# Two of eight experts for every token: rows sorted by expert through DRAM, in groups of 256, instead of every expert over every row

## The chip, the cores and the metric

The kernel runs on one core of a Trainium2 chip. A core has TensorE (PE in the profile; PEld is its weight load), VectorE (DVE), ScalarE (ACT), GpSimd (POOL) and SyncE (SP, which here only issues DMAs). The metric is the device time of one execution in microseconds (us), lower is better.

## What is computed

Four layers over a batch of 16 sequences of 256 tokens of width 128 (4096 rows, 32 tiles of 128 rows), each as x + layernorm(f(...)): a softmax attention, a block with a second softmax attention and a mixture of experts, an attention with second-power weights and decay, and a mixture with capacities. The change is about the mixture in the second layer (D = 128, hidden width F0 = 256, NE = 8 experts and a shared one):

```python
logits = h2 @ router_w
topw, topi = top_k(softmax(logits), 2);  topw = softmax(topw)
combine = sum(one_hot(topi, 8) * topw[..., None], axis=1)
shared = swiglu(h2, sh_gate, sh_up, sh_down)
gate = einsum('td,edf->etf', h2, e_gate);  up = einsum('td,edf->etf', h2, e_up)
eout = einsum('etf,efd->etd', silu(gate) * up, e_down)
moe_out = shared + einsum('etd,te->td', eout, combine)
```

`combine` is zero for six of the eight experts of every token.

## The kernel before

The program is one block per engine, each a list of steps written out by hand; engines meet only at semaphores, and nothing is reordered. There are five stages. `soft_layers` runs both softmax attentions, 32 steps of one sequence (tiles and semaphores end in S in the profile). `gated_layer` is the mixture above. `power_layer` is the third layer, 16 steps of 8 units, one head pair each (names end in P). `route` and `capped_mixture` are the last layer. A stage's first and last pieces are put into its neighbour's steps through tables of "guests": the key says after which step or unit, the value which piece. So the first steps of power (transposes, Q and K, the decays of sequences 0 and 1) are guests in the last part of the mixture, and the end of the mixture's last block is drained in power's first steps.

`gated_layer` before: 8 blocks (NBLK) of 512 rows. For a block the router's logits are formed and the two best experts found (`route`, small VectorE operations on 128x32 elements), then the block goes through all nine experts. The hidden width of an expert is cut in two chunks of 128, so a block has 18 units and the stage 144. A unit is:

- PE: three f16 matmuls of 512 columns into gate_ps and three into up_ps (each product of f32 numbers is made of three products of f16 halves, `PARTS`), L2121 and L2126. After both chunks of an expert, `down` (L2100) sends 24 f16 matmuls of 128 columns into down_ps.
- ACT: SiLU of gate_ps (gsg, L2187), later the high f16 half of the product (ghid, L2174).
- DVE: the product with up_ps (gprod, L2333), and per expert four additions weighted by `comb` (gacc, L2298).
- POOL: the low half (ghid, L2044).

At a block's end VectorE takes the layer norm's moments, GpSimd a power for the root (grs, L2039), VectorE applies it (gtmp, L2313) and adds to X. The weights of all experts are brought from DRAM, lifted and split in halves during `soft_layers` (27 pieces: gate, up and down of nine).

In `power_layer` the PE sends scores and decays of a unit (score_psP, decay_psP), VectorE takes the magnitude (AP, L1396, waits for the scores), ScalarE squares it and takes the decay's exponential, GpSimd multiplies the two (PTP, L982), and PE multiplies by V.

The last layer already uses indirect DMAs: GpSimd gathers token rows into xe by an index (L2442) and scatters results into expert_outputs (L2449), 128 rows each.

## Time and profile before

| | us |
|---|---|
| median of 3 runs | 1215.96 (1214.22 to 1217.85) |
| span of the profiled execution | 1221.8 |
| PE busy | 1117.0 |
| VectorE busy | 995.4 |
| ScalarE busy | 854.8 |
| GpSimd busy | 660.7 |

The profiled execution has a span of 1221.8 us, 5.8 us above the median of the timed runs; no other time of it is given, so this span is taken as its own time. Busy is the union of an engine's instructions. PE's busy time includes modelled ends, and the granted clock (1.00 is the full 2.4 GHz, 0.5 is 1.2 GHz) says how fast it was allowed to be.

### The profile page before, as it was taken

Reading aid. Unit: us, or ns where it says so; the run is one execution under the profiler, and the core shown is the slowest. Engines: PE = TensorE matmul, PEld = TensorE weight load, DVE = VectorE, ACT = ScalarE, POOL = GpSimd, SP = SyncE. Lnnn points to the kernel's source line nnn. Section 1 sums busy time; section 2 is a strip of 40 time slices with the busy share of each in tenths; the row PEclk is TensorE's granted clock in tenths of the full one; section 3 lists DMA queues with packets and bytes.
Section 4 is the critical chain, followed back from the end, with each engine's and each line's share of the span. In section 5 each row is a group of like instructions: output and inputs, shape, how many; then the busy total and the mean of one; then the engine's idle time right before and its main releaser. Section 6 shows DMA issues by size and latency. Waiting matters only on the chain. (4 is left out here: it accounts for less than half of the span.)

```text
span 1221.8 us, 33461 instructions
## 1 busy us (share of the span) xinstructions
PE 1117.0 (91%) x11750; PEld 627.2 (51%) x11750; DVE 995.4 (81%) x2706; ACT 854.8 (70%) x1830; POOL 660.7 (54%) x692
## 2 busy tenths in 40 slices
PE   5999999999999999999999999998999999947786
PEld 2344444444444444666656555555566665524552
DVE  4899999999899995788998889789899999771223
ACT  1788888888888887655555655688799998642214
POOL 3243344455333320666555666577788887725563
PEclk9999999999999998999999999999899999958998
DMA  4111111111111110000000000001212122041117
...
DMA packets 83459, 48.91 MB, mean 40 GB/s; under 512 B 17431, under 2 KB 80352, under 8 KB 83296
## 3 DMA queue, kind: packets, MB, share of 16 engines
...
## 5 line engine op out<-in xcount | busy, mean ns | idle before, releaser
L627 DVE TENSOR_REDUCE mxsS<-scoreS 128x2 f32<-128x512 f32 x512 | 328.6, 684 | 38.0 <-PE scoreS L766 32.7
L515 ACT ACTIVATE PTS<-stS 128x512 f32<-128x512 f32 x512 | 283.5, 591 | 52.6 <-PE stS L770 52.1
L2044 POOL TENSOR_TENSOR ghid<-gprod,ghid 128x512 f16<-128x512 f32 x144 | 165.7, 1158 | 141.4 <-ACT ghid L2174 140.3
L766 PE MATMUL scoreS<-QK 31*128 31x256 f16 x1024 | 173.3, 279 | 23.0 <-DVE mxsS L627 11.4
L982 POOL TENSOR_TENSOR PTP<-PTP,EP 128x512 f32<-128x512 f32 x128 | 163.2, 1286 | 51.0 <-ACT PTP L1210 50.9
L770 PE MATMUL stS<-QK 32*128 32x256 f16 x1024 | 169.6, 276 | 1.3 <-ACT PTS L515 1.3
L2174 ACT ACTIVATE ghid<-gprod 128x512 f16<-128x512 f32 x144 | 90.3, 627 | 94.8 <-DVE gprod L2333 94.0
L691 PE MATMUL pvS<-PTS,Vx 128*32 128x256 f32 x2048 | 140.3, 392 | 0.3
L1396 DVE TENSOR_SCALAR AP<-score_psP 128x768 int32<-128x768 int32 x128 | 121.5, 949 | 10.6 <-PE score_psP L1554 9.9
L766 PEld LDWEIGHTS scoreS<-QK 31*128 31x128 f16 x1024 | 53.8, 93 | 145.3 <-DVE mxsS L627 94.0
L1210 ACT ACTIVATE PTP<-AP,epsP 128x768 f32<-128x768 f32 x128 | 119.2, 932 | 7.1 <-DVE AP L1396 6.4
L388 POOL TENSOR_TENSOR rsS<-veS,halfS 128x2 f32<-128x2 f32 (+1 forms) x32 | 28.0, 874 | 171.1 <-DVE veS L595 90.6
L2121 PE MATMUL gate_ps<-ghT,split 128*128 128x512 f16 x432 | 116.9, 379 | 3.5 <-ACT gsg L2187 3.4
L2126 PE MATMUL up_ps<-ghT,split 128*128 128x512 f16 x432 | 116.8, 379 | 3.3 <-DVE gprod L2333 3.3
L2333 DVE TENSOR_TENSOR gprod<-gsg,up_ps 128x512 f32<-128x512 f32 x144 | 96.0, 681 | 23.2 <-ACT gsg L2187 18.1
L2100 PEld LDWEIGHTS down_ps<-split,ghid 128*128 128x128 f16 x1728 | 102.0, 98 | 17.6 <-issue 3.5
L2100 PE MATMUL down_ps<-split,ghid 128*128 128x128 f16 x1728 | 108.2, 219 | 0.0
L2187 ACT ACTIVATE gsg<-gate_ps 128x512 f32<-128x512 f32 x144 | 84.4, 586 | 28.0 <-PE gate_ps L2121 26.8
L1220 ACT ACTIVATE EP<-decay_psP 128x512 f32<-128x512 f32 x128 | 75.6, 591 | 20.1 <-PE decay_psP L1536 19.5
L691 PEld LDWEIGHTS pvS<-PTS,Vx 128*32 128x32 f32 x2048 | 54.1, 110 | 49.6 <-issue 21.9
L2126 PEld LDWEIGHTS up_ps<-ghT,split 128*128 128x128 f16 x432 | 41.4, 98 | 56.7 <-DVE gprod L2333 8.0
L2298 DVE SCALAR_TENSOR_TENSOR gacc<-down_ps,gcomb,gacc 128x128 f32<-128x128 f32 x224 | 62.6, 341 | 0.0
...
## 6 DMA issues: line engine op xcount, KB each, us to landing
...
tokens<-XB SPq DMA_DIRECT2D x16, 128.0 KB, 3.1
...
```

What stands on the lines that cost most here:

```text
L515: act.activation(PT[:, n % NPT, :], st_ps[:, (NS * t + n) % 3, :], ACT.Exp, scale=SCALE).then_inc(s_exp, 1)
L627: dve.tensor_reduce(mxs[:, u // 4, :, at], score_ps[:, n % 2, :].rearrange("p (c s) -> p c s", c=TC), AX.X, ALU.max).then_inc(s_max, 1)
L691: last = pe.matmul(pv_ps[32 * j:32 * j + 32, q], Vx[:, t % 3, c, 4 * g + j, :], PT[:, (4 * g + (j ^ 2)) % NPT, S * c:S * c + S], start=(c ...
L766: scored = pe.matmul(score_ps[:, k, cols], QK[part, new, g, 0, rows], QK[part, new, g, 1, :], start=True, stop=True)
L770: turned = pe.matmul(st_ps[:, (NS * t + n) % 3, cols], QK[part, old, g, 1, rows], QK[part, old, g, 0, :], start=True, stop=True)
L982: eng.tensor_tensor(w, w, E[:, n % NE, :], ALU.mult).then_inc(s_wd if n % NU in MULT_BY_DVE else s_wp, 1)
L1210: act.activation(PT[:, n % NW, :], A[:, n % NA, :], ACT.Square, bias=eps[:, 0:1]).then_inc(s_sq, 1)
L1396: dve.tensor_scalar(A[:, n % NA, :].bitcast(I32), score_ps[:, n % 2 * WU:n % 2 * WU + WU].bitcast(I32), 0x7FFFFFFF, None, ALU.bitwise_and) ...
L2044: pool.tensor_tensor(hid[:, n // FC % NHID, 1, c, :], prod[:, n % NPROD, :], hid[:, n // FC % NHID, 0, c, :], ALU.subtract).then_inc(s_hid, 1)
L2100: last = pe.matmul(down_ps[:, x % 2, t * D:(t + 1) * D], hid[:, x % NHID, lh, c, t * P:(t + 1) * P], down_w[:, lw, x % EX, c, :], start=(c ...
L2121: last = pe.matmul(gate_ps[:, n % 2, :], gate_w[:, lw, e, cols], hT[:, n // NQ % 2, lh, :], start=(k == 0), stop=(k == 2))
L2126: last = pe.matmul(up_ps[:, n % 3, :], up_w[:, lw, e, cols], hT[:, n // NQ % 2, lh, :], start=(k == 0), stop=(k == 2))
```

## The change

Blocks are now groups of 256 rows. The shared expert still runs over all rows in order: 16 units. For the eight others, each row is written twice to a DRAM table (`sorted0` for blocks 0 to 3, `sorted1` for 4 to 7), at a place that VectorE works out from the two chosen experts: rows of one expert stand together, and every expert begins at a multiple of 256. 4096 entries in up to 8 runs need at most 23 groups of 256, and all 23 are always run, for each half: 46 sorted units. So the stage has 62 units, each of 256 rows and the whole hidden width.

A sorted unit is loaded from the table by SyncE (gsin), transposed by PE (gturn_ps), split in halves by ScalarE and VectorE (ghTs), multiplied, and its result goes through ScalarE (gob) to the DRAM table `mixed`. Its expert is read by PE from SBUF into a register (TENSOR_LOAD), and the weights' addresses are computed from it with register instructions (ISA in the rows below). 64 indirect DMAs on GpSimd scatter the rows, 64 gather the results back, 8 for every block of 512 rows. VectorE then adds two results for every row with their weights. The third factor, `down`, is now f32 (weights not split, product not split), four f32 matmuls a unit.

The tables are first set to zero in 24 DMAs of up to 256 KB in the soft steps. The rows' scaling (squares, root, rows) moves to GpSimd in the soft steps 20 to 31, and the logits of blocks 0 to 3 and the first choice of experts into the last soft step. Blocks 0 to 3 are gathered and added in the mixture's last units (48 to 61), blocks 4 to 7 in power's steps 1 to 8.

On PE, in the middle of the mixture (gate_ps, up_ps and down_ps as above, split holds the f16 weights), two units of 128 hidden columns and 512 rows were:

```order
L2121 MATMUL gate_ps<-ghT,split 128x512 x3
L2126 MATMUL up_ps<-ghT,split 128x512 x3
L2121 MATMUL gate_ps<-ghT,split 128x512 x3
L2126 MATMUL up_ps<-ghT,split 128x512 x3
L2100 MATMUL down_ps<-split,ghid 128x128 x24
```

One sorted unit now is this, with down of the unit two before it and the transposes of the group two after it:

```order
L2233 TENSOR_LOAD gowner_139
L2233 ISA x2
L2295 ISA
L2295 MATMUL ggate_ps<-ghTs,split 128x256 x2
L2295 ISA
L2295 MATMUL ggate_ps<-ghTs,split 128x256
...
L2295 MATMUL gup_ps<-ghTs,split 128x256
L2263 ISA
L2263 MATMUL gdown_ps<-down_w,gprod 128x128
L2263 ISA
L2263 MATMUL gdown_ps<-down_w,gprod 128x128 x3
L2247 MATMUL gturn_ps<-cst,gsin 128x128 x2
```

Between the ISA rows stand in all 12 gate and up matmuls of 256 columns with 8 register instructions; with the load, its 2 and the 2 of down a unit has 13 instructions that were not there.

On POOL, at the mixture's end and in power's first two steps, stood (ghid is the low half, yP are power's rows):

```order
L2044 TENSOR_TENSOR ghid<-gprod,ghid 128x512 x10
L982 TENSOR_TENSOR PTP<-PTP,EP 128x512 x3
L1053 TENSOR_SCALAR yP<-X,mvP,rsP 128x128
L982 TENSOR_TENSOR PTP<-PTP,EP 128x512 x3
L1053 TENSOR_SCALAR yP<-X,mvP,rsP 128x128
L982 TENSOR_TENSOR PTP<-PTP,EP 128x512 x5
```

and now, from power's step 1 on, a gather stands after every second product:

```order
L2139 DMA ggot_late<-mixed,gidx_106 128x128
L975 TENSOR_TENSOR PTP<-PTP,EP 128x512 x2
L2139 DMA ggot_late<-mixed,gidx_106 128x128
L975 TENSOR_TENSOR PTP<-PTP,EP 128x512 x2
L1045 TENSOR_SCALAR yP<-X,mvP,rsP 128x128
L2139 DMA ggot_late<-mixed,gidx_106 128x128
L975 TENSOR_TENSOR PTP<-PTP,EP 128x512 x2
```

On POOL ahead of that, at the mixture's beginning, all 64 scatters stand in a row, with one root between them:

```order
L2128 DMA sorted<-gy,gidx_105 5888x128 x4
L2095 TENSOR_TENSOR girs<-gms,ghalf 128x4
L2128 DMA sorted<-gy,gidx_105 5888x128 x28
L2128 DMA sorted<-gy,gidx_106 5888x128 x32
```

The diff, cut to its core:

```diff
+MOE_PARTS = (4, 4)
+SLOTS = 256
...
+    SHARED, SORTED = NB, sum(groups)
+    UNITS = SHARED + SORTED
...
+        def expert(pe, n):
+            if n < SHARED:
+                return NE
+            h, j = group(n - SHARED)
+            if j == 0:
+                pe.wait_ge(s_rank, RANKED * (h + 1))
+            owners[n] = pe.value_load(owner[h][0:1, j:j + 1], min_val=0, max_val=NE)
+            return owners[n]
+
+        def columns(e, width, start, size):
+            if isinstance(e, int):
+                return slice(e * width + start, e * width + start + size)
+            return ds(e * width + start, size)
+
+        def sorted_turn(pe, s):
+            pe.wait_ge(s_sin[s % RING], 16 * (s // RING + 1))
...
+            reach(pe, s_slo, s)
+            for c in range(TC):
+                last = pe.transpose(turn_ps[:, c * P:(c + 1) * P], sin[:, s % RING, c, :], ident)
+            last.then_inc(s_sturn, 1)
 
         def down(pe, x):
-            pe.wait_ge(s_hid, FC * (x + 1))
+            pe.wait_ge(s_prod, x + 1)
...
+            for t in range(TC):
                 for c in range(FC):
-                    for k, (lh, lw) in enumerate(PARTS):
-                        last = pe.matmul(down_ps[:, x % 2, t * D:(t + 1) * D],
-                                         hid[:, x % NHID, lh, c, t * P:(t + 1) * P], down_w[:, lw, x % EX, c, :],
-                                         start=(c == 0 and k == 0), stop=(c == FC - 1 and k == 2))
+                    last = pe.matmul(down_ps[:, x % 2, t * D:(t + 1) * D],
+                                     prod[:, x % NPROD, c * SLOTS + t * P:c * SLOTS + (t + 1) * P],
+                                     down_flat[:, columns(e, FC * D, c * D, D)], start=(c == 0), stop=(c == FC - 1))
             last.then_inc(s_down, 1)
...
+            def hidden(n):
+                e = expert(pe, n)
+                if n < SHARED:
+                    pe.wait_ge(s_lo, n // 2 + 1)
+                else:
+                    pe.wait_ge(s_slo, n - SHARED + 1)
...
+                reach(pe, s_sg, n - 1)
+                for weight, ps, full in ((gate_w, gate_ps, s_gate), (up_w, up_ps, s_up)):
+                    if ps is up_ps:
+                        reach(pe, s_prod, n - 1)
+                    for c in range(FC):
+                        for k, (lw, lh) in enumerate(PAIRS):
...
+                            last = pe.matmul(ps[:, n % 2, c * SLOTS:(c + 1) * SLOTS],
+                                             weight[:, lw, columns(e, F0, c * P, P)], rows,
+                                             start=(k == 0), stop=(k == 2))
+                    last.then_inc(full, 1)
...
+        def scatter(pool, h, k):
+            c, t = k // len(tiles[h]), k % len(tiles[h])
+            if k == 0:
+                pool.wait_ge(s_zero, 3 + 16 * ZERO_PIECES)
+                pool.wait_ge(s_rank, RANKED * h + PLACED)
...
+            pool.indirect_dma_start(tables[h], bass.IndirectOffsetOnAxis(ap=idx[h][:, c, t:t + 1], axis=0),
+                                    y[:, tiles[h].start + t, :], None).then_inc(s_sorted[h], 16)
+
+        def gather(pool, b, k):
+            h, c, i = part_of_block(b), k // TB, k % TB
+            if k == 0:
+                stores(pool, h)
...
+            pool.indirect_dma_start(results_of(b)[:, c, i, :], None, results[h],
+                                    bass.IndirectOffsetOnAxis(ap=idx[h][:, c, t:t + 1], axis=0)).then_inc(arrival(b)[0], 16)
...
+        def add_shared(dve, x):
+            dve.wait_ge(s_down, x + 1)
+            a = XB[:, TC * x:TC * x + TC, :].rearrange("p c d -> p (c d)")
+            dve.scalar_tensor_tensor(a, down_ps[:, x % 2, 0:TC * D], 1.0 / LIFT, a, ALU.mult, ALU.add).then_inc(s_acc, 1)
+
+        def add_chosen(dve, b, c):
...
+            for i in range(TB):
+                t = b * TB + i
+                last = dve.scalar_tensor_tensor(XB[:, t, :], results_of(b)[:, c, i, :], W[:, c, t:t + 1], XB[:, t, :],
+                                                ALU.mult, ALU.add)
+            last.then_inc(s_sum, 1)
...
+            for n in range(UNITS):
+                if n < 4:
+                    soft.drain_vector(dve, n)
...
+                product(n)
...
+                if n == 2:
+                    rank(dve, 0)
+                if n == 14:
+                    choose(dve, 1)
+                if n == 16:
+                    rank(dve, 1)
...
+                if n >= SHARED - 1 and n + 2 < UNITS:
+                    sorted_low(n + 2 - SHARED)
...
+        def load(sp, s):
+            h, j = group(s)
+            if j == 0:
+                sp.wait_ge(s_sorted[h], 16 * 2 * len(tiles[h]))
...
+def groups_of(h):
+
+    return (2 * MOE_PARTS[h] * 512 + NE * (SLOTS - 1)) // SLOTS
```

`rank` is 13 VectorE operations on PE's running counts: each expert's number of rows, its first group, each row's place, and each group's expert.

## Rows read from the trace of the kernel before

**Rows 1.** The page: busy time by engine.
```profile
PE 1117.0 (91%) x11750; PEld 627.2 (51%) x11750; DVE 995.4 (81%) x2706; ACT 854.8 (70%) x1830; POOL 660.7 (54%) x692
```

**Rows 2.** Busy time in stretches: mixture, power, the last layer (busy us of each engine, clock).
```profile
486.00:793.00 307.00, 297.33 (x2708) 187.01 (x2704) 265.86 (x815) 182.24 (x358) 189.46 (x175) 1.00 0.02 4
793.00:1059.00 266.00, 257.84 (x3460) 155.59 (x3458) 240.72 (x574) 232.12 (x487) 213.53 (x196) 0.98 0.17 45
1059.00:1222.00 163.00, 111.83 (x578) 68.46 (x576) 63.24 (x294) 54.14 (x144) 78.20 (x85) 0.82 0.32 91
```

**Rows 3.** Who waited for whom, 486 to 793 us: total, times, longest.
```profile
PEld gate_ps L2121 <- ACT gsg L2187: 8.1, 11, 1.8
PEld up_ps L2126 <- DVE gprod L2333: 8.0, 10, 1.5
```

**Rows 4.** PE in order of time in the mixture: start, length, instruction, count.
```profile
485.96 0.82 PE L2121 MATMUL gate_ps<-ghT,split 128*128 128x512 f16 x3
...
494.90 1.50 PE L2100 MATMUL down_ps<-split,ghid 128*128 128x128 f16 x24
496.24 0.81 PE L2121 MATMUL gate_ps<-ghT,split 128*128 128x512 f16 x3
...
602.25 0.81 PE L2121 MATMUL gate_ps<-ghT,split 128*128 128x512 f16 x3
602.90 0.81 PE L2126 MATMUL up_ps<-ghT,split 128*128 128x512 f16 x3
...
792.75 0.38 PE L1519 MATMUL decay_psP<-cstb 128*128 128x512 bf16 x1
```

**Rows 5.** The chain that ended last: f32 matmuls and a gather's landing.
```profile
1110.75 2.40 DMA xe<-tokens,idx_in
...
1137.43 3.57 PE cps L2496 x32
```

**Rows 6.** Groups of instructions of the whole trace: count, busy us, mean ns.
```profile
L2333 DVE TENSOR_TENSOR gprod<-gsg,up_ps 128x512 f32<-128x512 f32 x144 | 96.0, 681 | 23.2 <-ACT gsg L2187 18.1 <-PE up_ps L2126 3.3 <-DVE gsel L2253 0.4
L2187 ACT ACTIVATE gsg<-gate_ps 128x512 f32<-128x512 f32 x144 | 84.4, 586 | 28.0 <-PE gate_ps L2121 26.8
L714 PE MATMUL miscS<-cst,yS 128*128 128x128 f32 x64 | 14.7, 314 | 0.7 <-DVE router L1728 0.7
L604 DVE SCALAR_TENSOR_TENSOR HLS<-miscS,bq,HLS 128x256 f16<-128x256 f32 x16 | 7.6, 475 | 2.7 <-ACT HLS L486 2.7
```

**Rows 7.** GpSimd in order of time: indirect DMAs, with the idle time ahead of each.
```profile
1109.50 0.94 POOL L2442 DMA_INDIRECT xe<-tokens,idx_in  x1 [0.30 <-issue]
1110.75 0.94 POOL L2442 DMA_INDIRECT xe<-tokens,idx_in  x1 [0.30 <-issue]
```

**Rows 8.** DMA issues: count, size, us to landing.
```profile
experts<-in_L_ffn_e_gate_dram SPq DMA_DIRECT2D x8, 128.0 KB, 2.3
```

**Rows 9.** VectorE in order of time, the third product of the mixture.
```profile
490.87 0.69 DVE L2333 TENSOR_TENSOR gprod<-gsg,up_ps 128x512 f32<-128x512 f32 x1 [0.91 <-ACT gsg L2187]
```

**Rows 10.** Busy time in power's steps 1 to 4 and 5 to 8.
```profile
809.60:876.00 66.40, 60.68 (x807) 36.21 (x807) 60.78 (x143) 55.17 (x111) 52.38 (x48) 0.95 0.15 41
876.00:942.40 66.40, 65.83 (x881) 41.13 (x880) 60.88 (x151) 59.16 (x131) 53.73 (x51) 0.97 0.20 53
```

**Rows 11.** Lines 1323 and 2241: durations in ns, least, median, most.
```profile
L1323 DVE TENSOR_TENSOR ynP<-farP,rcP x16: 291/426/1187, 827.0 to 1070.5; 128x128 f32<-128x128 f32 x16
L1323 DVE TENSOR_TENSOR ynP<-misc_bP,rcP x15: 290/291/292, 823.6 to 1058.4; 128x128 f32<-128x128 f32 x15
...
L2241 DVE TENSOR_TENSOR gsc<-gsc,cst x8: 181/990/991, 480.2 to 744.7; 128x32 f32<-128x32 f32 x8
```

**Rows 12.** Groups in power's steps 0 to 8: count, busy us, mean ns.
```profile
L982 POOL TENSOR_TENSOR PTP<-PTP,EP 128x512 f32<-128x512 f32 x68 | 86.7, 1285 | 30.9 <-ACT PTP L1210 30.7
L2039 POOL TENSOR_TENSOR grs<-gve,ghalf 128x4 f32<-128x4 f32 x1 | 1.0, 1025 | 0.0
...
L2313 DVE TENSOR_SCALAR gtmp<-gacc,gmv,grs 128x128 f32<-128x128 f32 x4 | 2.3, 578 | 0.0
L2298 DVE SCALAR_TENSOR_TENSOR gacc<-down_ps,gcomb,gacc 128x128 f32<-128x128 f32 x8 | 2.2, 336 | 0.0
```

**Rows 13.** Busy time in the second half of the soft stage.
```profile
250.00:460.00 210.00, 202.71 (x2374) 98.91 (x2370) 193.89 (x443) 181.81 (x398) 77.95 (x99) 1.00 0.17 40
```

1110 lines of the change are left out of this document (646 added, 464 removed).

## The prediction

> **What bounds the kernel now.** I read the page first, then the stretches, then the mixture's waits and PE's own order in it. The page has PE busy for 1117.0 of 1221.8 us [rows 1], but the three stretches behind the soft stage differ: in the mixture PE is busy 297 of 307 us, while ScalarE and GpSimd are busy 182 and 189 [rows 2]. The longest waits of PE there sum to 16 us [rows 3]. So the mixture is bound by PE's columns. Its length is from the first gate_ps at 485.96 to power's first matmul at 792.75, 306.8 us [rows 4]. Three matmuls of 512 columns pass in 0.65 us and 24 of 128 columns in 1.34 us (494.90 to 496.24) [rows 4], that is 217 and 56 ns each, with the weight loads hidden. One of the 144 units costs 6 x 0.217 + 12 x 0.056 = 1.97 us, all of them 284 us; the other 23 us are seven blocks' transposes and logits, power's first guests and waits. In power, the reader should see three engines close together: PE 257.8, VectorE 240.7, ScalarE 232.1 of 266 us, GpSimd 213.5 [rows 2]. What leaves the mixture for power does not fall on an idle engine.
>
> **The change: PE's units.** A matmul of 256 columns is bounded by the two rows at 56 and 217 ns [rows 4]; by its columns it is 0.109. Gate and up have 12: 1.31 us. Down is four f32 matmuls of 128 columns, eight records; 32 such records passed in 3.57 us, 0.112 each [rows 5]: 0.90. A shared unit is 2.21 us. A sorted unit has two f32 transposes more, 64 of which took 14.7 us, 0.23 each [rows 6]: 2.67 us of array time. 16 x 2.21 + 46 x 2.67 = 158 us against 284: the columns saved are worth 126 us. It is that little because 46 groups are always run, where two experts a row would fill 32.
>
> **The register instructions.** No row shows one. Below, they are bounded by nothing: the 22 matmuls and 22 weight loads of a sorted unit need at most 1.23 us to issue, at the 28 ns an instruction that the 48 of down show (1.34 us for 24 pairs [rows 4]), so 13 register instructions hide beside 2.67 us as long as each takes under 0.11. Above, the nearest row of an instruction that fetches something before it can go is GpSimd's 0.30 us of issue ahead of each indirect DMA [rows 7]: 1.23 + 13 x 0.30 = 5.1 us a unit. They can't overlap waits much, since several carry the unit's semaphore waits. I take 0.13 each, near the lower end since twelve of thirteen read no memory, so a sorted unit is 1.23 + 1.69 = 2.92 us. The first transfer to a register is the one that may be long.
>
> The Trainium skill (DMA: Bandwidth & Descriptors, "Latency and other measured facts") gives a floor of about 600 ns for such a load of a register from a tensor. With the other twelve at 0.11 an estimate by that page would be 3.2 us a unit, some 11 us more in all. No row here shows it.
>
> **The start: GpSimd's scatters.** Let G be the time of the first gate_ps. PE has 16 shared units less two downs that come later (33.6), the fronts of four blocks (four transposes and 12 tiny matmuls, at most 0.92 + 0.67, so 6.4) and 1 us of the soft stage's drain: it is through at G + 41. The third product ended at 490.87 + 0.69, G + 5.6 [rows 9]; behind it stand 12 steps of rank, each like a small VectorE operation of 181 to 990 ns [rows 11], which I put at 0.28: G + 9. Then GpSimd issues 32 scatters, one every 1.25 us (1109.50 to 1110.75 [rows 7]), with a root of 1.0 [rows 12] between: the last goes at G + 49. A gather landed 2.40 us after its issue [rows 5], a load of 128 KB takes 2.3 [rows 8], two transposes and two halves 1.4 (0.48 for the low half [rows 6]). The first sorted unit starts at G + 55. PE waits 14 us. The second half's scatters start when rank(1) is done, about G + 62, end at G + 102 and are ready at G + 108; PE comes there after 23 units, at G + 122. They are hidden by the first half's units, and cost nothing unless these shrink below 2.3 us.
>
> **The end: GpSimd's gathers.** The last result of the first half is stored three units late, about G + 131. 32 gathers are 40 us, the roots and power's first rows 8, waits inside 4: G + 183. PE comes to unit 60, which needs the last of them, at about G + 190. Covered, by 7 us; at 2.67 us a unit by nearly nothing, so PE can't gain all of its own speed.
>
> Mixture: 55 + 46 x 2.92 = 189, and for power's guests and their waits 13 as now (306.8 less 283.7 of units and 7 x 1.6 of fronts, plus the two downs that are drained later): 202. Saved: 104 us.
>
> VectorE and ScalarE have room in it: per sorted unit 0.68 + 0.48 and 0.59 + 2 x 0.4 us [rows 6].
>
> **Power's steps 1 to 8.** These took 132.8 us, with GpSimd busy 52.4 + 53.7 and VectorE 60.8 + 60.9 [rows 10]. GpSimd gets 32 gathers of 1.25 and four roots, less the one of before: 106 + 43 = 149 us. VectorE loses about 5 us of block 7's moments and norm (gtmp alone is 2.3 [rows 12]) and gets this four times, and 32 additions. An addition of before is 0.34 us [rows 12], but it read PSUM; the new one reads two operands from SBUF. Line 1323 shows both kinds: from PSUM 290 to 292 ns, with both in SBUF 291 to 1187, median 426 [rows 11]. For each block I take 2.7 + 1.5: 122 - 5 + 4 x 9.2 = 154 us. Neither fits in 132.8. At the 97 to 99% that the busiest engine reaches (PE 65.8 of 66.4 [rows 10]), 158 us: lost 25. If the additions never wait it is 14, if each does for 0.9 us, 45.
>
> **The soft stage.** Four blocks' fronts for one on PE, 4.8 us. VectorE's six sums of squares (0.68 each, as gprod of the same shape [rows 6]) go to an engine busy 194 of 210 us and mostly fit [rows 13]; the zeroing DMAs fit, since nothing waits for them there. Nine weight pieces fewer on ScalarE and GpSimd give nothing: PE, at 203 of 210, is the bound. Lost: 5 us.
>
> The last layer is as before, with weights brought later, under power's last steps.
>
> Sum: -104 + 25 + 5 = -74. From the profiled 1221.8, 1148; the median of the runs is 5.8 lower, so **1142 us**. Own range: 1116 (2.67 us a unit less what the gathers hold back, power at 14, a shorter stall) to 1165.
>
> **Rivals.** (a) Registers free and power cheap: 1110 to 1116, as just worked out. For it, PE's issue of 28 ns an instruction; against it, the engines' sums in power. (b) Registers at 0.17 to 0.25 us: units of 3.4 to 4.5 us, 1166 to 1215. (c) GpSimd's issue slows under load. All 28 + 28 indirect DMAs of before ran with VectorE busy 63 of 163 us [rows 2]; now it is busy 80% and more beside them. At 2.0 us each the first stall grows by 24 and power by 18: 1184. The second kind of line 1323 [rows 11] says that the two engines do get in each other's way. The Trainium skill (SBUF — State Buffer, "SBUF: two separate sides") says that a VectorE operation that takes the shared port pair keeps GpSimd from writing its descriptors. By that rule the DMAs' own durations would stretch, and not only VectorE's; no row here shows it. (d) Slower than before: register instructions at the issue gap, 0.30 us each, nothing hidden. 46 x (5.13 - 2.92) = 102: 1244 us. It decides from 0.25 us each on, where a unit is 4.5 us. Against it, only one in thirteen reads memory. (e) The columns are saved but PE falls to 1.2 GHz whenever it waits: in power's steps 1 to 4 the clock was 0.95 with PE busy 91% [rows 10]. With PE at 84% there and a 14 us stall in the mixture it may cost 5 to 15 us, inside the range.
>
> **Numbers.** Forecast with (e) 0.5, (a) 0.12, (b) 0.14, (c) 0.12, (d) 0.1, else 0.02. The range 1112 to 1190 leaves out (d), half of (b)'s upper part and a part of (a). A difference of 0.3%, 4 us, is what can be told here. Faster 0.87, same 0.02, slower 0.11.
>
> **What would show it.** In the profile after: gate_ps to gate_ps of neighbouring sorted units 2.9 us apart, with PE's gaps marked as issue; a wait of about 14 us at unit 16 for a DMA, with GpSimd's 32 scatters 1.25 us apart ahead of it; the whole mixture near 202 us; power's steps 1 to 8 near 158 us with GpSimd and VectorE over 93% busy and PE waiting for them. I'd be wrong if units were over 3.5 us, if the indirect DMAs stood over 1.5 us apart, or if a step of power stayed at 16.6 us.

## The result and the profile after

The changed kernel takes **1180.9 us** (median of 4 runs, 1178.53 to 1187.95), the kernel before, run beside it, 1215.1 (4 runs, 1213.49 to 1217.85): a ratio of 0.972, 95% interval 0.968 to 0.976. It is faster, as forecast, and inside the range, but by 34 us where 74 had been forecast.

The profiled execution took 1178.53 us, its span is 1176.7. The page has this row in place of [rows 1]:

```profile
PE 1030.3 (88%) x10524; PEld 615.7 (52%) x10524; DVE 887.7 (75%) x2262; ACT 757.2 (64%) x1638; POOL 644.3 (55%) x707
```

PE lost 1226 matmuls and 87 us of busy time. Busy time in stretches, in the columns of [rows 2]: the mixture, the power layer, and the piece from power's step 15 to the end:

```profile
501.00:699.00 198.00, 165.28 (x1460) 149.35 (x1458) 115.24 (x300) 79.68 (x182) 112.00 (x122) 0.93 0.33 96
703.00:968.00 265.00, 244.87 (x2620) 143.78 (x2624) 227.24 (x538) 185.91 (x385) 206.48 (x189) 0.76 0.16 42
1012.00:1177.00 165.00, 119.13 (x779) 74.26 (x778) 75.65 (x320) 66.03 (x165) 88.30 (x94) 0.84 0.34 96
```

The column behind the engines is the clock that TensorE was granted: in power it was 0.98 before [rows 2] and is 0.76 now. PE in order of time, as in [rows 4]:

```profile
500.82 0.83 PE L2295 MATMUL ggate_ps<-hTf,split 128*128 128x256 f16 x6
...
542.41 0.82 PE L2295 MATMUL ggate_ps<-hTf,split 128*128 128x256 f16 x6
...
546.64 0.70 PE L2208 MATMUL gfront_ps<-gmask,gones 128*128 128x128 bf16 x16
559.29 0.69 PE L2247 MATMUL gturn_ps<-cst,gsin 128*128 128x128 f32 x2 [11.95 <-DMA gsin<-sorted]
561.15 0.66 PE L2247 MATMUL gturn_ps<-cst,gsin 128*128 128x128 f32 x2 [1.18 <-DVE ghTs L2549]
562.25 1.46 PE L2295 MATMUL ggate_ps<-ghTs,split 128*128 128x256 f16 x6 [0.43 <-issue]
...
601.98 0.82 PE L2295 MATMUL ggate_ps<-ghTs,split 128*128 128x256 f16 x6
...
604.40 0.82 PE L2295 MATMUL ggate_ps<-ghTs,split 128*128 128x256 f16 x6
...
699.10 0.58 PE L1519 MATMUL decay_psP<-cstb 128*128 128x512 bf16 x1 [0.42 <-DMA MP<-partsP]
```

The reader should see the mixture's two ends, 500.82 and 699.10; a sorted unit every 2.42 us (601.98 to 604.40) with no gap; and the stall ahead of the first sorted unit, 542.41 to 562.25. GpSimd's first scatters, which that stall waits for:

```profile
514.55 1.22 POOL L2128 DMA_INDIRECT sorted<-gy,gidx  x1 [0.18 <-issue]
516.08 0.96 POOL L2128 DMA_INDIRECT sorted<-gy,gidx  x1 [0.30 <-issue]
517.35 0.96 POOL L2128 DMA_INDIRECT sorted<-gy,gidx  x1 [0.31 <-issue]
```

Where the time went, from the marks of [rows 4] and the starts of power's steps (a step is timed from VectorE's first operation on score_ps). The second profile of the kernel before is the experiment before_again:

| stretch, us | before | before, second profile | after |
|---|---|---|---|
| up to the first gate_ps | 486.0 | 492.3 | 500.8 |
| mixture | 306.8 | 306.3 | 198.3 |
| power, to the start of step 15 | 252.0 | 251.0 | 313.1 |
| step 15 to the end | 177.0 | 165.2 | 164.5 |
| span | 1221.8 | 1214.8 | 1176.7 |

Against the first profile that is +14.8, -108.5, +61.1 and -12.5, together -45.1; against the second +8.5, -108.0, +62.1 and -0.7, together -38.1. The mixture gave what was forecast; power took back more than half of it.

**Power's steps 0 to 11**, the stretch that all experiments are compared in. The kernel before, then the kernel after:

```profile
795.40:994.80 199.40, 191.43 (x2556) 116.69 (x2554) 182.41 (x438) 175.07 (x373) 162.09 (x150) 0.97 0.17 46
```
```profile
703.00:962.20 259.20, 239.07 (x2540) 140.19 (x2540) 221.55 (x521) 180.68 (x375) 200.90 (x185) 0.76 0.16 42
```

TensorE runs the same matmuls (the counts differ by records that are missing). It is busy with them for 47.6 us more and waits 12.2 us more (20.1 for 8.0): four fifths of the 59.8 us stand in its busy time, with the granted clock at 0.76 in place of 0.97, that is, with more of the matmuls at the lower of its two clock levels, 1.2 GHz. That says where the time stands, and not what a held clock would give back. Steps 12 to 14 have none of the new work and take 50.0 us in both.

### The profile page after: what moved, and what is told of

The parts are those of the page before. It is cut to its first block and busy times, and to the rows that moved or that the text cites. A ratio compares the mean times of both kernels' runs of the same rounds, so it can differ in the third digit from the quotient of the medians.

```text
span 1176.7 us, 30894 instructions
## 1 busy us (share of the span) xinstructions
PE 1030.3 (88%) x10524; PEld 615.7 (52%) x10524; DVE 887.7 (75%) x2262; ACT 757.2 (64%) x1638; POOL 644.3 (55%) x707
## 5 line engine op out<-in xcount | busy, mean ns | idle before, releaser
L760 PE MATMUL scoreS<-QK 31*128 31x256 f16 x1024 | 171.3, 280 | 33.5 <-DVE mxsS L621 14.8
L1396 DVE TENSOR_SCALAR AP<-score_psP 128x768 int32<-128x768 int32 x128 | 121.7, 951 | 21.6 <-PE score_psP L1555 20.6
L2128 POOL DMA_INDIRECT sorted<-gy,gidx x64 | 61.6, 963 | 32.6 <-issue 32.6
L2263 PE MATMUL gdown_ps<-down_w,gprod 128*128 (+1 forms) x496 | 68.4, 284 | 2.1 <-issue 1.1
L2361 ACT ACTIVATE ghTs<-gturn_ps,norm 128x256 f16<-128x256 f32 x46 | 21.8, 474 | 74.7 <-PE gturn_ps L2247 74.7
L2263 PEld LDWEIGHTS gdown_ps<-down_w,gprod 128*128 128x128 f32 x496 | 62.9, 199 | 3.8 <-issue 3.0
L2545 DVE TENSOR_TENSOR gprod<-gsg,gup_ps 128x512 f32<-128x512 f32 x62 | 42.6, 686 | 25.1 <-PE gup_ps L2295 19.1
L1541 PE MATMUL score_psP<-QK 31*128 31x128 f16 x512 | 58.3, 242 | 0.0
L1537 PE MATMUL decay_psP<-MP 32*128 32x128 bf16 x512 | 58.2, 242 | 0.0
L1520 PE MATMUL decay_psP<-cstb 128*128 128x512 bf16 x128 | 57.9, 452 | 0.0
L2356 ACT ACTIVATE gsg<-ggate_ps 128x512 f32<-128x512 f32 x62 | 37.1, 598 | 30.5 <-PE ggate_ps L2295 30.5
L1555 PE MATMUL score_psP<-QK 31*128 31x128 f16 x256 | 39.9, 241 | 18.8 <-DVE AP L1396 18.0
```

The source lines that it names most:

```text
L760: scored = pe.matmul(score_ps[:, k, cols], QK[part, new, g, 0, rows], QK[part, new, g, 1, :], start=True, stop=True)
L1396: dve.tensor_scalar(A[:, n % NA, :].bitcast(I32), score_ps[:, n % 2 * WU:n % 2 * WU + WU].bitcast(I32), 0x7FFFFFFF, None, ALU.bitwise_and) ...
L1541: pe.matmul(score_ps[:, o:o + P], QK[band, t % 3, g, 1, rows], QK[band, t % 3, g, 0, rows], start=True, stop=True)
L2128: pool.indirect_dma_start(tables[h], bass.IndirectOffsetOnAxis(ap=idx[h][:, c, t:t + 1], axis=0), y[:, tiles[h].start + t, :], None).then_ ...
L2263: last = pe.matmul(down_ps[:, x % 2, t * D:(t + 1) * D], prod[:, x % NPROD, c * SLOTS + t * P:c * SLOTS + (t + 1) * P], down_flat[:, colum ...
```

## The experiments

The table has power's steps 0 to 11 of every kernel: their length, TensorE's busy time and waits in it, its mean granted clock, VectorE's busy time, and "excess", which is worked out from the trace: by how much VectorE's operations were longer than the shortest of their line and shape in the whole trace, summed where it is over 0.15 us. Runs with an interval had three rounds, the others one execution; each ratio is to the kernel before as it ran beside that kernel. The length of these steps differs between single executions by more than small effects: static and zero_act change nothing in power and have 248.3 and 259.6 us, the kernel after 259.2. Differences under some 11 us between two lengths are no evidence by themselves.

| kernel | run, us | ratio to before, 95% | length | PE busy | PE waits | clock | VectorE | excess |
|---|---|---|---|---|---|---|---|---|
| before | 1215.1 | 1 | 199.4 | 191.4 | 8.0 | 0.97 | 182.4 | 12.1 |
| before_again | 1216.6 | | 198.4 | 191.5 | 6.9 | 0.97 | 181.6 | 11.3 |
| after | 1180.9 | 0.972 (0.968 to 0.976) | 259.2 | 239.1 | 20.1 | 0.76 | 221.6 | 31.1 |
| fill1 | 1187.1 | 0.973 (0.965 to 0.980) | 267.4 | 242.0 | 25.4 | 0.84 | 225.8 | 33.5 |
| fill2 | 1174.2 | 0.964 (0.956 to 0.972) | 250.8 | 235.7 | 15.1 | 0.96 | 219.1 | 26.9 |
| fill_odd | 1181.0 | 0.973 (0.967 to 0.979) | 252.0 | 236.3 | 15.7 | 0.91 | 220.4 | 29.7 |
| no_late | 1156.3 | | 234.5 | 214.9 | 19.6 | 0.86 | 199.4 | 16.0 |
| no_gather | 1172.9 | | 251.0 | 232.8 | 18.2 | 0.79 | 211.4 | 20.6 |
| no_add | 1182.4 | | 256.2 | 237.2 | 19.0 | 0.76 | 210.0 | 26.0 |
| spread | 1198.7 | 0.982 (0.977 to 0.987) | 271.0 | 240.1 | 30.9 | 0.76 | 228.2 | 38.0 |
| spread_fill | 1200.3 | 0.986 (0.983 to 0.990) | 272.4 | 245.7 | 26.7 | 0.90 | 230.5 | 39.9 |
| before_burst | 1231.3 | | 219.8 | 205.5 | 14.3 | 0.90 | 198.4 | 20.2 |
| before_gather | 1231.9 | | 214.0 | 201.1 | 12.9 | 0.92 | 192.2 | 21.5 |
| zero_act | 1170.1 | 0.962 (0.958 to 0.967) | 259.6 | 237.9 | 21.8 | 0.76 | 217.7 | 27.0 |
| zero_fill | 1163.1 | 0.959 (0.953 to 0.965) | 249.4 | 234.2 | 15.2 | 0.96 | 219.2 | 27.1 |
| zero_fill_os | 1168.8 | 0.960 (0.955 to 0.966) | 263.3 | 241.4 | 21.9 | 0.93 | 222.2 | 37.2 |
| light | 1167.8 | 0.960 (0.955 to 0.965) | 256.3 | 232.2 | 24.1 | 0.79 | 225.1 | 34.1 |
| light_fill | 1167.3 | 0.959 (0.955 to 0.964) | 255.3 | 238.2 | 17.1 | 0.94 | 225.3 | 33.1 |
| half_scatter | 1174.1 | | 259.9 | 234.7 | 25.2 | 0.78 | 223.4 | 33.0 |
| static | 1166.4 | | 248.3 | 223.4 | 24.9 | 0.82 | 217.4 | 26.9 |

A correction to texts below: block b's additions stand in power step 2b-5 and its normalization in 2b-4, so for the late blocks 4 to 7 in steps 3, 5, 7, 9 and 4, 6, 8, 10; the gathers in 2b-7 and 2b-6, steps 1 to 8. Only step 11 has no work of its own, and it shows: 16.1 us in the kernel after. Step 0 has the additions of block 3.

### Clock or occupation: fill1, fill2, no_late

fill1 adds one matmul of 512 columns to each unit of the affected steps, fill2 two:

```
-                for _ in range(AGAIN if t >= NB - 2 else t == 0):
+                for _ in range(AGAIN if t >= NB - 2 else t <= 11):               # fill1
+                for _ in range(AGAIN if t >= NB - 2 or t <= 11 else 0):          # fill2
```

> One more matmul of 512 columns per unit (0.22 us, its result is overwritten) in power's steps 1 to 11; nothing is left out. Clock theory: the 61 us lost in power are mainly TensorE running at 1.2 GHz after it has waited for VectorE; the extra work keeps it busy, time at 1.2 GHz in power falls from 133 us to under 60, steps 4 to 11 fall from 20 to 27 us to 17 to 20, and the kernel is 15 to 35 us faster than the changed one (1145 to 1165). Occupation theory: VectorE and GpSimd set the steps, the clock only follows; the extra matmuls change nothing or cost up to 20 us (1180 to 1200).

> Two more such matmuls per unit in power's steps 0 to 11. Clock theory: hardly any time at 1.2 GHz in power, but 3.5 us of TensorE a step more, so steps that VectorE does not fill (9 to 11) take 18 to 20 us: 1150 to 1170. Occupation theory: TensorE's work now passes that of VectorE, 1195 to 1225.

no_late drops the late blocks' gathers and keeps one column of their additions:

```
             t = (b - first_block[h]) * TB + i
+            if b >= first_block[1]:
+                return
             pool.indirect_dma_start(results_of(b)[:, c, i, :], None, results[h], ...)
...
+                if b >= first_block[1]:
+                    last = dve.scalar_tensor_tensor(XB[:, t, 0:1], XB[:, t, 0:1], W[:, c, t:t + 1], XB[:, t, 0:1], ...)
+                    break
```

> Leaves out the 32 gathers of blocks 4 to 7 and all but one column of their additions, so the chosen experts' results are missing in half the rows; moments and norm of these blocks stay in power. Clock theory and occupation theory both expect a large gain in steps 1 to 8; the clock theory expects steps 9 to 11 to be 16 us too, since they were slow without any work of their own, power near 275 us in all and the kernel at 1125 to 1140. If steps 9 to 11 stay at 20 to 25 us, what slows them is something else.

Steps 0 to 11 of fill2, then of no_late:

```profile
705.60:956.40 250.80, 235.67 (x2723) 128.89 (x2721) 219.09 (x522) 180.50 (x376) 201.51 (x186) 0.96 0.17 44
```
```profile
705.80:940.30 234.50, 214.85 (x2541) 128.43 (x2540) 199.40 (x498) 177.99 (x375) 166.40 (x153) 0.86 0.14 37
```

fill2 brings the clock back to 0.96. Its 183 matmuls more, at the 0.217 us of [rows 4], are 40 us of TensorE; what is left of its busy time is 196, where 191 is the kernel before. So TensorE's own matmuls took 43 us less and the fillers 40 more; the length fell by 8, which one execution can't show. The run of 1174.2 is between the ranges of both theories, and its interval overlaps that of the change. fill1 holds the clock half way and gains nothing that can be told (1187.1, as the theory of occupation had it). Neither run gives the price of the clock alone, since the fillers take TensorE's time.

no_late takes 25 of the 60 us, and its run of 1156.3 missed the range of 1125 to 1140. The clock still falls without that work (0.86), and 35 of the 60 us stay. Block 3's additions in step 0 and all blocks' moments and normalization stand there still; no run leaves them out, so what the 35 us are is not shown.

### Which engine: no_gather and no_add

no_gather leaves out the gathers only (the additions read the token row itself), no_add reduces the additions only.

> The 32 late gathers (blocks 4 to 7) are left out, their additions stay and read the token row itself: GpSimd has 8 issues of about 1.25 us fewer per block, VectorE as much work as in the changed kernel. Theory A: the slow steps 3, 5, 7 stay at 23 to 27 us and the run at 1170 to 1181 us. Theory C (GpSimd): steps as in no_late, 16 to 22 us, and 1153 to 1160 us.

> The 32 late gathers stay, their additions are reduced to one column: VectorE is relieved of 8 additions a block, GpSimd not. Theory A: as no_late, 1153 to 1162 us. Theory C: as the changed kernel, 1175 to 1185 us.

```profile
705.40:956.40 251.00, 232.82 (x2540) 137.00 (x2540) 211.37 (x522) 179.36 (x375) 167.53 (x153) 0.79 0.13 35
```
```profile
710.10:966.30 256.20, 237.21 (x2540) 139.16 (x2538) 209.99 (x498) 179.63 (x375) 200.38 (x185) 0.76 0.16 42
```

no_gather's run of 1172.9 is in theory A's range and no_add's of 1182.4 in theory C's, so neither alone is the cause: without the gathers 8 us go, without the additions 3, without both 25. The 8 and the 3 are too small for single executions; that the two don't add up to 25 is the reading. In no_add the steps with four gathers still take 17 to 27 us, with GpSimd busy up to 21 of 27; in no_gather a step with additions takes 20.2 with VectorE busy 20.0, and the step behind it up to 25.9 at a clock of 0.53. The kernel after has the same in steps 9 and 10:

```profile
901.40:921.50 20.10, 17.56 (x235) 10.66 (x238) 19.86 (x56) 15.41 (x34) 14.10 (x13) 0.97 0.12 32
921.50:946.10 24.60, 24.60 (x210) 14.50 (x210) 17.38 (x44) 15.70 (x34) 15.46 (x14) 0.54 0.09 24
```

TensorE waits for 2.5 us in step 9; the low clock comes in step 10, where it waits for nothing and is busy for the whole of 24.6 us.

no_add shows a second thing. Its VectorE executes as many operations as no_late's (x498), of the same sizes, and is busy 10.6 us longer. The operations themselves are longer. The kernel after, VectorE and GpSimd in order of time in step 7:

```profile
852.64 1.04 POOL L2139 DMA_INDIRECT ggot_late<-mixed,gidx  x1 [0.16 <-ACT PTP L1204]
852.66 0.30 DVE L1332 TENSOR_TENSOR farP<-misc_bP,farP 128x144 f32<-128x144 f32 x1
852.99 0.25 DVE L1319 RECIPROCAL rcP<-farP 128x16 f32<-128x16 f32 x1
853.28 3.08 DVE L1321 TENSOR_TENSOR ynP<-farP,rcP 128x128 f32<-128x128 f32 x1
...
853.70 2.49 POOL L975 TENSOR_TENSOR PTP<-PTP,EP 128x512 f32<-128x512 f32 x2
```

The operation onto yn reads both operands from SBUF; its twin that reads PSUM takes 0.29 every time [rows 11]. Here it takes 3.08 us and ends at 856.36, just behind GpSimd's gather and **two** products (852.64 to 856.19). Beside it the operation of 852.66, which reads PSUM, is not stretched. [rows 11] has the same line at up to 1.19 us in the kernel before, one product's length. The Trainium skill (SBUF — State Buffer, "Who interferes with whom") says that a VectorE operation with both inputs in SBUF and a GpSimd one that reads SBUF exclude each other for a whole instruction. The trace agrees, and goes further: here VectorE did not get its turn between three GpSimd instructions in a row.

### Each cost by itself in the kernel before: before_burst, before_gather

Steps 7 and 11 of the kernel before are steady at 16.1 us. before_burst gives VectorE 16 operations more in each:

```
+                    if t in (7, 11) and u % 2 == 1:
+                        for i in range(4):
+                            dve.scalar_tensor_tensor(spare[:, i, :], cst[:, 0:P], cst[:, 0:1], cst[:, 0:P], ALU.mult, ALU.add)
```

> The kernel before, with 16 extra VectorE operations of 128x128 (onto a tile of their own) in each of the power steps 7 and 11, four ahead of units 1, 3, 5 and 7; both steps lie in its steady part, where a step takes 16.1 us with VectorE busy 15.2 and TensorE 16.0 at 2.4 GHz. The additions take about 0.35 us each, so VectorE has 20.8 us of work in such a step. Theory of the clock: the step gets 4 to 6 us longer by the wait, TensorE's granted clock falls, and with it this or the next step gets another 4 to 9 us, so 8 to 15 us for each of the two bursts and 16 to 30 us in the run (1232 to 1246). Theory of occupation alone: 20.8 to 21.5 us for the step, 16.1 for the next, 10 us in the run (1225).

before_gather gives GpSimd four gathers more in each:

```
+                    if t in (7, 11) and u % 2 == 1:
+                        ...
+                        pool.indirect_dma_start(spare[:, u // 2, :], None, dram["L0_ffn_wo"],
+                                                bass.IndirectOffsetOnAxis(ap=first_row[:, 0:1], axis=0))...
```

> The kernel before, with four extra indirect gathers of 128 rows on GpSimd in each of the power steps 7 and 11 (ahead of the products of units 1, 3, 5, 7, into tiles of their own); VectorE and TensorE get no work more. GpSimd has 14.0 us of work in such a step of 16.1, plus 4 x 1.25 = 19.0. Theory of the shared way into SBUF: GpSimd comes behind, its products run back to back, VectorE's operations with two SBUF operands stretch (from 0.3 to 1 to 3 us each), so VectorE's busy time in the step grows from 15.2 to 17 to 19 us without an operation more, and the step takes 19 to 24 us. Theory that GpSimd's products are buffered and that only VectorE's own work counts: the step stays at 16.1 to 17 and VectorE at 15.2.

before_burst, step 6 and step 7; then before_gather, step 6 and step 7:

```profile
897.10:913.20 16.10, 16.00 (x221) 9.95 (x220) 15.38 (x41) 15.19 (x35) 14.19 (x15) 1.00 0.22 54
913.20:939.70 26.50, 22.97 (x221) 13.41 (x220) 23.19 (x56) 16.80 (x36) 15.88 (x15) 0.68 0.15 38
```
```profile
903.90:920.00 16.10, 16.00 (x221) 9.94 (x220) 15.36 (x40) 15.19 (x35) 14.17 (x15) 1.00 0.19 52
920.00:942.70 22.70, 19.80 (x221) 12.03 (x220) 19.54 (x39) 15.92 (x36) 19.98 (x19) 0.77 0.30 57
```

Each burst costs 10.4 us, in its own step; the next is 16.0 again. VectorE gets 8 us more, of which 5.5 are the 16 operations at their shortest (0.34) and the rest excess; TensorE waits 3.4 us more, and is busy 7.0 more at a clock of 0.68. That is the theory of the clock, 8 to 15 us a burst, with a run of 1231.3 just under its range. The four gathers cost 6.6 us (the second time 7.0), and the VectorE column is the point: with not one operation more it rises from 15.4 to 19.5 (17 to 19 had been expected, and 19 to 24 us for the step). From the trace of that step, in order of time:

```profile
925.87 0.99 POOL L1093 DMA_INDIRECT spareP<-in_L_ffn_wo_dram,first_rowP  x1 [0.16 <-issue]
...
926.23 3.43 DVE L1285 TENSOR_TENSOR partsP<-restP,partsP 16x256 bf16<-16x256 f32 x1
...
926.88 2.48 POOL L986 TENSOR_TENSOR PTP<-PTP,EP 128x512 f32<-128x512 f32 x2
```

This is the same picture as in the kernel after, produced by gathers alone. In step 11 of the same run it was the operation of L1283, a cast that reads one operand from SBUF: 3.34 us where its shortest is 0.28, again across a gather and two products. So it isn't only the operations with two. The theory that only VectorE's own work counts is out.

These prices can't be added up for the change. Eight steps with four gathers at 6.8 and four with 8 additions at half a burst, 5.2, would be 75 us; no_late took out just this work, and 25 us went. What a gather or an addition costs in a step that is already slow is less than in a steady one.

### Three tries at relief: spread, fill_odd, light, each with its filled twin

spread puts one tile's addition in each unit of the step, and moments and normalization in the next (with GpSimd's root two units later):

```
-                    after.update({(t, 3): tail(("add0", b)), (t, 5): tail(("add1", b)), (t, 7): tail(("moments", b)),
-                                  (t + 1, 3): tail(("apply", b))})
+                    after.update({(t, u): tail((f"tile{u}", b)) for u in range(8)})
+                    after.update({(t + 1, 1): tail(("moments", b)), (t + 1, 5): tail(("apply", b))})
```

> The late additions one tile per unit over all eight units of steps 3, 5, 7, 9, the moments in unit 1 and the normalization in unit 5 of the step behind; nothing is left out. Theory A (VectorE's burst): VectorE is busy 22.8 us of step 7 and 17.0 of step 8 (39.8 for the pair, against 30.4 for a pair of the kernel before), so steps 3 to 10, which took 186.9 us in the changed kernel, can come down toward 4 x 39.8 = 159; expected 165 to 175, a run of 1160 to 1171 us, and pairs of like steps (20 and 21 us) in place of 26 and 21. Theory B (the sum of the work on VectorE counts, however it lies, and TensorE's clock follows the waits): steps 3 to 10 stay at 180 to 190 and the run at 1176 to 1188. Theory C (GpSimd's gathers hold up the products): as B.

> As spread, and two extra matmuls in each unit of power steps 0 to 10, as in fill2. If the clock still falls with the additions spread (theory A with the clock as a second cause), this takes another 5 to 10 us: 1150 to 1163 us. If spreading alone keeps TensorE at 2.4 GHz, the filler costs what it did in step 11 of fill2 (2.8 us a step where TensorE is the bound, less where VectorE is): 0 to 10 us slower than spread. Theory B: 1170 to 1180, as fill2.

Theory A is out: steps 3 to 10 take 186.1 us (187.0 in the kernel after), as B and C had it, which this run can't tell apart. But at 1198.7 the run missed every range. It is slower than the kernel after by 18, by a later start of power (711.0 for 703.0) and by steps 1 and 11, which are 7 us longer each, step 11 at a clock of 0.64. Why the clock falls there is not shown. Excess grew to 38.0; that operations in more places meet GpSimd more often fits this, and is not tested. spread_fill ran at 1200.3, with the clock at 0.90, excess at 39.9 and steps 3 to 10 at 191.3. That is out of the ranges of theories A and B; it is 2 us above spread, as in the third case, but that case had the clock held without fillers, and it was not. On this placement two fillers a unit gained nothing.

fill_odd puts three matmuls a unit where VectorE is the bound and one elsewhere:

```
-                for _ in range(AGAIN if t >= NB - 2 else t == 0):
+                for _ in range(AGAIN if t >= NB - 2 else 3 if t in (3, 5, 7, 9) else int(t <= 10)):
```

> The changed kernel with three extra matmuls in each unit of steps 3, 5, 7 and 9 (where VectorE is the bound) and one in the others up to 10. In steps 0 to 11 TensorE's busy time grew from 191.4 to 239.1 us with the same matmuls and its waits from 8.0 to 20.1; fill2 took back the clock (busy 235.7) but its 183 extra matmuls cost 39 us. If the fillers of the odd steps go into time that VectorE takes anyway (steps of 22.5 to 24.5) and one holds the clock in the even ones (17.4 to 18.5), steps 3 to 10 take 160 to 170 us and the run 1160 to 1172. If the clock falls in the even steps, as in fill1: 1178 to 1190.

Steps 3 to 10 take 175.1 us, no better than fill2's 174.3 and outside the 160 to 170 hoped for; the run of 1181.0 is that of the kernel after and lies in the second range. The clock was 1.00 in steps 4 and 10 and 0.84 and 0.85 in 6 and 8. A filler placed by the bound isn't better than an even one.

light takes work off GpSimd (and has zero_act's edit, below):

```
-                    if u == 4 and has(t + 3):
+                    if u == 4 and has(t + 3) and t not in LIGHT:
                         normalized(pool, t + 3, 0)
...
+            def normal(t, c):
+                act.activation(y[:, c, :], batch_rows(t)[c], ACT.Identity, bias=nm[:, c:c + 1], scale=rs[:, c:c + 1])...
```

> zero_act, and in power steps 1 to 9 the two normalizations of incoming rows and the two of outgoing rows (128x128, 0.86 to 0.95 us each on GpSimd) are done by ScalarE with a bias that VectorE makes (two tiny operations a step, 0.15 us each); nothing is left out. GpSimd's work in a step with four gathers falls from 19.0 to 15.4 us, under the 16.1 of TensorE. If GpSimd's being behind is what stretches VectorE's operations: stretched time (29.5 us more than in the kernel before over steps 0 to 11) halves at least, steps 3 to 10 take 160 to 172 us instead of 183, and the run 1148 to 1162. If VectorE's work or the clock alone decide: within 5 us of zero_act's 1170.

> light with two extra matmuls in each unit of power steps 0 to 11. Beside zero_fill's 1163.1. If GpSimd's being behind sets the addition steps: steps 3 to 10 (24.2, 18.9, 24.7, 18.9, 24.6, 18.9, 21.3, 21.2 in zero_fill) come to 20 to 22 and 18.9, 8 to 16 us less: 1147 to 1156 us. If not: 1160 to 1167.

The 29.5 us in the text of light were counted by another rule; by that of the table the excess grew by 19.0 us (31.1 for 12.1). light, steps 0 to 11:

```profile
692.80:949.10 256.30, 232.19 (x2540) 136.22 (x2540) 225.09 (x538) 191.94 (x409) 172.42 (x151) 0.79 0.16 42
```

GpSimd is relieved by 29 us (zero_act has 201.0), and the excess does not fall: 34.1, where zero_act has 27.0. The run is 1167.8 for zero_act's 1170.1, not 1148 to 1162, and light_fill is not under zero_fill. So relieving GpSimd over a whole step does not shorten VectorE's operations, and that part of the theory falls. In both long operations shown above a gather and two products stood back to back; that this order decides it is argued from them, not tested.

### The soft stage: zero_act

```
-                soft.sync(sp, {2 + k: functools.partial(gated.zeroed, sp, k) for k in range(ZERO_PIECES)})
+                soft.sync(sp, {})
...
+                soft.scalar(act, {**{(2 + k, 3): functools.partial(gated.zeroed, act, k) for k in range(ZERO_PIECES)}, ...
```

> The changed kernel with its 22 zeroing transfers started from ScalarE's queue in place of SyncE's; all else as it was. Start of the mixture was 14.8 us later than in the kernel before (500.8 and 486.0), 9.3 of it by the end of step 19, in which time the zeroing runs. Theory A (the small shift and spread transfers of QK queue behind the 256 KB ones of SyncE): 6 to 10 us of it go, mixture's start at 491 to 495 and a run 5 to 12 us under the changed kernel's, if the power steps don't change. Theory B (16 DMA engines are busy with the zeroing, whatever queue it comes from): the start stays at 499 to 502. Theory C (ScalarE pays for the issues, 22 x 0.1 us or more): 500 to 506.

TensorE's waits for the small transfers onto QK, 0 to 465 us (total, times, longest): before, after, zero_act.

```profile
PE scoreS L766 <- DMA QK<-nmS: 7.0, 10, 1.2
```
```profile
PE scoreS L760 <- DMA QK<-nmS: 14.4, 17, 1.5
```
```profile
PE scoreS L760 <- DMA QK<-nmS: 6.4, 13, 1.2
```

Theory A: the waits are back at what they were before, and the mixture starts 9.7 us earlier:

```profile
491.15 0.83 PE L2295 MATMUL ggate_ps<-hTf,split 128*128 128x256 f16 x6
```

This is no chance of one execution: in the eleven kernels that zero from SyncE the mixture starts at 499.2 to 505.3 us, in the five that zero from ScalarE at 489.2 to 491.6, and in the kernel before and its variants at 485.6 to 492.3. The bytes are the same; the small transfers on SyncE's queue had waited for the 256 KB ones ahead of them in that queue. The Trainium skill (DMA: Bandwidth & Descriptors, "Queues, rings and completion order") says that a DMA engine takes turns between the queues that it has work for; the trace agrees, since the transfers moved to another queue and the waits went. The run is 1170.1, a ratio of 0.962 to the kernel before. zero_twice, the changed kernel with each zeroing transfer started twice, was meant for the same question and has no result.

### The first stall and the registers: half_scatter, static

half_scatter leaves out the second choice's 16 scatters of the first half; static takes the expert's number from the program instead of a register:

```
-            moved(0, range(4, 2 * len(tiles[0])))
+            moved(0, range(4, len(tiles[0])))                                    # half_scatter
...
-            owners[n] = pe.value_load(owner[h][0:1, j:j + 1], min_val=0, max_val=NE)
+            owners[n] = (n - SHARED) % NE                                        # static
```

> The 16 scatters of the second choice of the first half are left out (those rows of the sorted table stay zero), so the first table is whole about 20 us earlier; the transfers of the table, the units and everything behind stay. If the scatters at 1.26 us each make TensorE wait 17.6 us before unit 16: that wait goes to 0 to 2 us, the mixture takes 179 to 184 us instead of 198.3, and the run 1160 to 1170. If the table's own transfer or the ranking sets it: wait and mixture as they were.

> The expert of a sorted group comes from a fixed number instead of a register loaded from SBUF (the groups get a wrong expert's weights; work and order are the same). The sorted units took 2.42 us each with register loads of about 0.3 us on TensorE's queue. If those are hidden, as the back-to-back matmuls say: 2.40 to 2.42 us per unit and a run within 5 us of the changed kernel's. If a part shows: 2.1 to 2.35 us per unit, 3 to 14 us over 46 units.

half_scatter, PE: the last shared unit and the first sorted one:

```profile
546.92 0.82 PE L2295 MATMUL ggate_ps<-hTf,split 128*128 128x256 f16 x6
554.37 1.46 PE L2295 MATMUL ggate_ps<-ghTs,split 128*128 128x256 f16 x6 [0.46 <-issue]
```

7.45 us between them where the kernel after has 19.84: 12.4 us of the stall were scatters, not all of it. What is left is led by the chain of ranking and count (TensorE waits 1.7 us for gmask) and the turn of the first rows (three waits, 3.0 us). The mixture took 188.0 us, not 179 to 184. The run is one execution at 1174.1, above its range, with a soft stage 4.6 us longer than that of the kernel after, and says little by itself.

static, PE:

```profile
603.13 0.82 PE L2295 MATMUL ggate_ps<-ghTs,split 128*128 128x256 f16 x6
...
605.55 0.82 PE L2295 MATMUL ggate_ps<-ghTs,split 128*128 128x256 f16 x6
```

2.42 us a unit, as with registers, whose load shows in the kernel after, from the group that reads gowner (count, least/median/most in ns):

```profile
L2233 PEldq TENSOR_LOAD <-gowner x46: 296/305/511, 561.2 to 688.9; - x46
```

A load of 0.3 us is hidden entirely by the matmuls already queued. static's run of 1166.4 is outside its range of 5 us, and by its steps (248.3 us for 259.2) that comes from power, which holds no register: TensorE is busy there 15.7 us less at a clock of 0.82. It is the scatter from one execution to the next, and the size of doubt on every single run here. The Trainium skill (DMA: Bandwidth & Descriptors, "Latency and other measured facts") gives about 600 ns for such a load; here it was 305.

### The last layer: before_again

> The kernel before as it is, for a second profile. In its first one TensorE's instructions in the last layer come 0.70 us apart in two stretches (1127.9 to 1136.8 and 1148.6 to 1158.4 us), and from step 15 to the end it takes 177.0 us, where the four kernels with the change take 164.2 to 165.7. If this belongs to the program (something of its code or its transfers there): again 175 to 178 us and the same stretches. If it is a chance of one execution: 164 to 168 us, and a run about 10 us under the first one's 1215 to 1222.

From step 15 to the end, the first profile of the kernel before, then the second:

```profile
1044.80:1221.80 177.00, 126.03 (x777) 76.09 (x776) 74.67 (x320) 65.65 (x164) 88.55 (x94) 0.84 0.30 84
```
```profile
1049.60:1214.80 165.20, 119.46 (x777) 73.98 (x777) 75.59 (x320) 65.89 (x164) 88.18 (x94) 0.84 0.31 90
```

The 12.5 us were a chance of one execution, and no gain of the change. The run was no faster for it (1216.6), since its mixture started 6.3 us later. What slowed TensorE's instructions to one in 0.70 us there stays open. The forecast took 5.8 us off for the distance of that execution to the median, so about half of it was allowed for.

### The best version: zero_fill, zero_fill_os

> zero_act and fill2 together: zeroing from ScalarE's queue (start of the mixture 9.6 us earlier) and two extra matmuls in each unit of power steps 0 to 11. If the two causes are independent, their gains add: fill2 took 6.8 us off the changed kernel's 1180.9, zero_act 10.8, so 1160 to 1167 us. If the fillers' gain was chance: 1168 to 1175.

zero_fill takes **1163.1 us** (1160.67 to 1171.53), 0.959 of the kernel before, the lowest median and in its expected range. Its interval (0.953 to 0.965) lies below that of the change (0.968 to 0.976), but overlaps that of zero_act (0.958 to 0.967): the queue's gain is shown, and that the fillers add to it is likely and not shown. Its steps 0 to 11, and those of zero_fill_os, which also moves four copies of sums from VectorE to ScalarE in each addition step:

```
+                    if t in ON_SCALAR and u in (1, 3, 4, 7):
+                        sums(t if u == 7 else t - 1, {7: 0, 1: 1, 3: 2, 4: 3}[u])
```

> As zero_fill, and the four copies of sums (128x384, 0.55 us each) of each of the power steps 3, 5, 7 and 9 go from VectorE to ScalarE; nothing is left out. If VectorE's work (22.8 us in such a step) sets the length of these steps, each gets 1.5 to 2.5 us shorter: 6 to 10 us under zero_fill. If GpSimd's gathers or the clock set them, as no_add and spread make it look: within 3 us of zero_fill.

```profile
692.80:942.20 249.40, 234.24 (x2723) 128.22 (x2721) 219.16 (x522) 180.65 (x376) 201.49 (x186) 0.96 0.17 44
```
```profile
694.30:957.60 263.30, 241.42 (x2723) 131.80 (x2723) 222.20 (x505) 185.99 (x392) 203.21 (x186) 0.93 0.15 41
```

The ratios are the same, 0.959 and 0.960. VectorE lost copies worth 9 us and is busy 3 us longer: what was freed is filled by excess (37.2 for 27.1). The addition steps 3, 5, 7 and 9 do get shorter, 90.3 us for 94.8, and steps 4, 6, 8 and 10 longer, 94.2 for 77.9. The run is 5.7 us longer in its median, neither the 6 to 10 less nor within 3.

## Why the prediction was partly right

**The mixture: right sum, wrong terms.** 198.3 us for 202. Registers were put at 1.69 us of a unit; they cost nothing (static), and rival (a)'s mechanism holds for them. A sorted unit is 2.42, not 2.92, and not 2.67 either: its two transposes take 0.22 together (604.18 to 604.40), not 0.23 each. That is 23 us over 46 units. Against it stand two costs that were put too low. The first sorted unit starts at G + 61.4, not G + 55: the scatters begin at G + 13.7, not G + 9, since rank ended at 512.3 and GpSimd first had the last block's squares; they were issued at 1.26 us each as forecast. And from unit 16 on the 46 units take 136.9 us (562.25 to 699.10), of which 25.5 are not units: waits for power's first rows and a low clock, for which 13 had been put. -23 + 6.4 + 12.5 is -4.

**Power: the step that failed.** "At the 97 to 99% that the busiest engine reaches, 158 us: lost 25" was 60. Power's steps 1 to 8, before and after, in the columns of [rows 2]:

```profile
810.30:946.60 136.30, 130.29 (x1743) 79.96 (x1742) 124.94 (x300) 117.77 (x251) 109.61 (x102) 0.96 0.18 47
```
```profile
724.10:901.40 177.30, 160.27 (x1743) 94.97 (x1742) 153.14 (x353) 121.65 (x252) 146.70 (x136) 0.77 0.18 48
```

The forecast had VectorE at 154 us and GpSimd at 149; they are 153.1 and 146.7. What failed is the step from there to the time: VectorE was not busy 97 to 99% of these steps but 86%. TensorE, left out of that sum, is busy 160.3 with the matmuls that took it 130.3 before, at a clock of 0.77 for 0.96, and the steps are 177.3 long, not 158. Rival (e) had seen the clock, at 5 to 15 us; in steps 0 to 11 TensorE's busy time grew by 47.6 of the 59.8. In before_gather and before_burst waits longer by 2.8 and 3.4 us in a step came with 3.8 and 7.0 more of matmul time, where nothing else had changed for TensorE. What the clock alone is worth in the changed kernel is not shown, since its waits stand in the same steps.

The steps named were wrong too: blocks 4 to 7 are added up to step 9 and normalized up to step 10, and block 3 is added in step 0. Steps 0, 9 and 10 are 19 us longer than before, 8.5 of it in step 10, where TensorE waits for nothing. The base of 132.8 was eight mean steps; steps 1 to 8 had taken 136.3.

That VectorE's sum came out is in part luck. Its excess was priced at 1.5 us a block, for additions alone. The 32 late additions did have the 6.0 us of it, but over steps 0 to 11 the excess grew by 19.0: ynP (L1321) rose from 3.3 to 10.2 and partsP (L1265 and L1267) from nothing to 4.7, operations that had been there before. Part of the blocks' own work went to steps 9 and 10 and made up for it in the sum. Gathers alone bring such excess about (before_gather). The lower end of power, 14 us, is too low by the forecast's own rule: GpSimd's 149 us at 97 to 99% make it some 19.

**The soft stage.** "the zeroing DMAs fit, since nothing waits for them there" was wrong: nothing waits for them, but small transfers stood behind them in their queue. 8.5 to 14.8 us for 5, of which zero_act gives back 9.7.

**The last layer** is as before, as forecast.

**Rivals.** (b) and (d), registers, are out. (c) had the right pair of engines and the wrong victim: the scatters took 0.96 us each, 1.26 apart, and the late gathers 1.04 (medians), for 0.94 in [rows 7], with VectorE busy beside them, and it was VectorE that stood still. The sum from the terms as measured, against the second profile: -108.0 + 62.1 + 8.5 - 0.7 = -38.1, where -74 was forecast; power's term alone accounts for the difference. Open are why the clock falls in one step and not in another like it, why it does so differently from run to run, and the 35 us of power that stay without the late gathers and additions.
